# Edge stage of a two-layer graph network: layers spread in eight steps over two rounds, edge batches taken singly by TensorE

## What is computed

```python
def _L0_gnn_ref(node_feats, src, dst, eps, W1, b1, W2, b2, gamma, beta):
    neigh = segment_sum(node_feats[src], dst, num_segments=n)
    h = (1.0 + eps) * node_feats + neigh
    h = relu(h @ W1 + b1) @ W2 + b2          # 256 -> 512 -> 256
    mean, var = h.mean(axis=0), square(h - mean).mean(axis=0)
    return (h - mean) * rsqrt(var + BN_EPS) * gamma + beta
```

## Time and profile before

| | |
|---|---|
| median of three runs | 2266.91 us |
| the profiled execution | 2265.84 us |
| its span | 2264.3 us |
| TensorE matmuls busy / weight loads busy | 93% / 87% |
| VectorE / ScalarE / GpSimd busy | 73% / 54% / 25% |
| edge stage, from the first batch to the last layer | 150.6 to 602 us |

### The profile page before, as it was taken

The page is one execution under the profiler, slowest core; times in us unless marked ns, Lnnn a source line. Parts: engine busy times, 40 slices in busy tenths (PEclk is TensorE's granted clock), DMA queues, the critical chain, the costliest instruction groups (busy, mean ns, idle before and its releaser), DMA issues. The chain is left out here.

```text
span 2264.3 us, 47270 instructions
## 1 busy us (share of the span) xinstructions
PE 2094.6 (93%) x18287; PEld 1966.4 (87%) x18287; DVE 1653.3 (73%) x3119; ACT 1233.8 (54%) x2875; POOL 569.9 (25%) x406
## 2 busy tenths in 40 slices
PE   5559999999879999998999999999999999999996
PEld 3348999999769999997778999899988999999996
DVE  6888877778388888885657655556657867888885
ACT  5565555555437676675533444444435336677674
POOL 3000000000016777773000000000000014777775
PEclk9789999999989999999999999999999999999998
DMA  3413333333547778776001666366651025777776
GB/s 122 142 59 105 102 89 89 112 95 89 160 157 217 222 225 240 222 225 169 20 25 50 184 194 188 98 196 188 188 156 63 20 92 173 226 225 237 232 220 170
DMA packets 241114, 339.04 MB, mean 150 GB/s; under 512 B 33407, under 2 KB 202546, under 8 KB 240754
## 3 DMA queue, kind: packets, MB, share of 16 engines
q1 hardware_dynamic: 208908, 296.19, 41.6%
q0 software_dynamic: 28528, 35.76, 8.5%
q10 hardware_dynamic: 3446, 3.97, 0.5%
HBM read 258.89 MB, written 76.95 MB: 148 GB/s over the span
## 5 line engine op out<-in xcount | busy, mean ns | idle before, releaser
L1977 POOL DMA_INDIRECT SC<-xd,slot_i x128 | 186.5, 1457 | 1461.3 <-DVE slot_q L1613 1332.4
L2371 PE MATMUL bank<-WB_r,XN_r 128*128 128x448 f32 x1400 | 399.7, 367 | 3.7 <-DVE WB_r L2330 3.7
L2330 DVE TENSOR_TENSOR WB_r<-WB,WB_r 128x448 fp32r<-128x448 f32 x350 | 214.0, 624 | 166.1 <-ACT WB_r L2323 166.1
L2323 ACT CAST WB_r<-WB 128x448 fp32r<-128x448 f32 x350 | 197.6, 568 | 222.2 <-PE bank L2371 219.1
L2371 PEld LDWEIGHTS bank<-WB_r,XN_r 128*128 128x128 f32 x1400 | 263.2, 188 | 26.8 <-DVE wb__r L2296 4.4
L1907 PE MATMUL bank<-SC_r,WB_r 128*128 128x256 f32 (+1 forms) x2064 | 250.7, 280 | 8.2 <-issue 7.4
L1907 PEld LDWEIGHTS bank<-SC_r,WB_r 128*128 128x128 f32 x2064 | 244.0, 188 | 12.7 <-issue 12.7
L1048 ACT CAST WB_r<-bank 128x200 fp32r<-128x200 f32 x391 | 140.5, 359 | 194.7 <-PE bank L1032 193.4
L1922 PE MATMUL bank<-R_r,H_r 128*128 128x256 f32 x1752 | 215.1, 282 | 4.8 <-DVE R_r L1818 4.8
L1922 PEld LDWEIGHTS bank<-R_r,H_r 128*128 128x128 f32 x1752 | 208.9, 189 | 5.1 <-issue 5.1
L1770 ACT ACTIVATE wb_<-bank,WB 128x256 f32<-128x256 f32 (+1 forms) x344 | 133.2, 476 | 80.0 <-PE bank L1907 41.3
(11 more groups left out here) (463 smaller groups left out, 5130.4 us busy)
## 6 DMA issues: line engine op xcount, KB each, us to landing
WB<-adjw SPq DMA_DIRECT2D x350, 224.0 KB, 2.9
WB<-in_f_pack SPq DMA_DIRECT2D x127, 512.0 KB
WB<-in_f_pack SPq DMA_DIRECT2D x62, 640.0 KB
adjw<-X SPq DMA_DIRECT2D x24, 1600.0 KB, 7.5
WB<-in_f_pack SPq DMA_DIRECT2D x65, 516.0 KB
xd<-XN SPq DMA_DIRECT2D x15, 640.0 KB, 5.5
y<-X SPq DMA_DIRECT2D x10, 640.0 KB, 3.3
X<-y SPq DMA_DIRECT2D x6, 640.0 KB, 6.5
```

Of the source, the lines that this page charges most:

```text
L1977: e.indirect_dma_start(yin[i % 2][:, q * D:(q + 1) * D], None, XD, bass.IndirectOffsetOnAxis(ap=slot_i[:, 2 * i + q:2 * i + q + 1], axis=0 ...
L2323: e.copy(split_w(m)[0], RAW[m % PR]).then_inc(S("whigh"), 1)
L2330: e.tensor_tensor(al, RAW[m % PR], ah.bitcast(F32), ALU.subtract).then_inc(S("wlow"), 1)
L2371: mm_ = e.matmul(conv_bank(k, band, c)[:, 0:PW], x[st][:, o], y, start=(st == 0 and i == 0), stop=(st == T - 1 and i == 2))
```

## The change

TensorE takes a batch in front of each sums slot, in place of two in front of every other slot. The sixteen matmuls of the layers of a pair of rounds come in eight steps of two: a step of `layer1_pe` behind slots 3, 5 and 7 of the odd round and slot 0 of the next, a step of `layer2_pe` behind slots 3, 5 and 7 of that round and slot 0 of the one after. `layer2_pe` now goes through the four hidden blocks outside and the two output halves inside, so its first two steps need only the first two hidden blocks. `layer1_act` comes in two halves, the second a round later; `layer2_act` and `stats_dve` come a round later.

```diff
-    def layer2_pe(e, q):
+    def layer2_pe(e, q, hc):
         o = pair_cols(q)
         w = o.stop - o.start
-        e.wait_ge(S("lay"), 6 * q + 4)
+        e.wait_ge(S("lay"), 6 * q + (2 if hc < 2 else 4))
         for c in range(2):
-            for hc in range(4):
-                m = e.matmul(B[6][:, c * 256:c * 256 + w], w2[:, hc, c * 128:(c + 1) * 128], hidden[:, hc, 0:w],
-                             start=(c == 0 and hc == 0), stop=(hc == 3), skip_group_check=True)
-        m.then_inc(S("layT"), 1)
+            m = e.matmul(B[6][:, c * 256:c * 256 + w], w2[:, hc, c * 128:(c + 1) * 128], hidden[:, hc, 0:w],
+                         start=(c == 0 and hc == 0), stop=(hc == 3), skip_group_check=True)
+        if hc == 3:
+            m.then_inc(S("layT"), 1)
...
+    PARTS_AT = ((0, 3), (0, 5), (0, 7), (1, 0), (1, 3), (1, 5), (1, 7), (2, 0))
+
+    def layers_pe(e, b, i):
+        for part, (later, at) in enumerate(PARTS_AT):
+            if at == i and layers_at(b - later) is not None:
+                (layer1_pe if part < 4 else layer2_pe)(e, layers_at(b - later), part % 4)
...
     def count_pe(e):
-        for b in range(T + 3):
+        for b in range(T + 5):
             for i in range(8):
-                for j in (i, i + 1) if i % 2 == 0 else ():
+                for j in (i,):
                     if has_batch(b, j):
                         hots_pe(e, 8 * b + j)
                 if i == 1 and 2 <= b < T + 2:
                     turn_sums_pe(e, b - 2)
                 if 1 <= b <= T:
                     sums_pe(e, b - 1, i)
-                if i == 5 and layers_at(b) is not None:
-                    layer1_pe(e, layers_at(b))
-                if i == 7 and layers_at(b) is not None:
-                    layer2_pe(e, layers_at(b))
+                layers_pe(e, b, i)
...
-                if i == 1 and b and layers_at(b - 1) is not None:
-                    layer2_act(e, layers_at(b - 1))
+                if i == 1 and layers_at(b - 2) is not None:
+                    layer2_act(e, layers_at(b - 2))
                 if i == 6 and layers_at(b) is not None:
-                    layer1_act(e, layers_at(b))
+                    layer1_act(e, layers_at(b), 0)
+                if i == 1 and layers_at(b - 1) is not None:
+                    layer1_act(e, layers_at(b - 1), 1)
...
-                if i == 5 and b and layers_at(b - 1) is not None:
-                    stats_dve(e, layers_at(b - 1))
+                if i == 6 and layers_at(b - 2) is not None:
+                    stats_dve(e, layers_at(b - 2))
```

More of the change, by code:

```diff
@@ L1117, in pair_cols, with layer1_pe @@
         return slice(256 * q, min(256 * q + 256, NP))
-    def layer1_pe(e, q):
+    def layer1_pe(e, q, hc):
         o = pair_cols(q)
         w = o.stop - o.start
[L1122 to L1127, removed]
-        for hc in range(4):
[L1129 to L1132, removed]
-                m.then_inc(S("layT"), 1)
@@ L1135, in layer2_pe @@
-    def layer2_pe(e, q):
+        if hc == 0:
+            e.wait_ge(S("gadd"), min(2 * q + 2, T))
+            if q:
+                e.wait_ge(S("lay"), 6 * q)
+            else:
+                e.wait_ge(S("w_late"), W_LATE)
+                e.wait_ge(S("key16"), dve_step(FILLS - 1, 0))
+        for c in range(2):
+            m = e.matmul(B[6 + hc // 2][:, hc % 2 * 256:hc % 2 * 256 + w], w1[:, c, hc * 128:(hc + 1) * 128], XT[:, c, o],
+                         start=(hc % 2 == 0 and c == 0), stop=(c == 1), skip_group_check=True)
@@ L1136, in layer2_pe @@
+        if hc % 2:
+            m.then_inc(S("layT"), 1)
+    def layer2_pe(e, q, hc):
         o = pair_cols(q)
         w = o.stop - o.start
-        e.wait_ge(S("lay"), 6 * q + 4)
+        e.wait_ge(S("lay"), 6 * q + (2 if hc < 2 else 4))
         for c in range(2):
-            for hc in range(4):
-                m = e.matmul(B[6][:, c * 256:c * 256 + w], w2[:, hc, c * 128:(c + 1) * 128], hidden[:, hc, 0:w],
-                             start=(c == 0 and hc == 0), stop=(hc == 3), skip_group_check=True)
@@ L1143, in layer2_pe, with layer1_act @@
-        m.then_inc(S("layT"), 1)
-    def layer1_act(e, q):
+            m = e.matmul(B[6][:, c * 256:c * 256 + w], w2[:, hc, c * 128:(c + 1) * 128], hidden[:, hc, 0:w],
+                         start=(c == 0 and hc == 0), stop=(hc == 3), skip_group_check=True)
+        if hc == 3:
+            m.then_inc(S("layT"), 1)
+    def layer1_act(e, q, half):
         w = pair_cols(q).stop - pair_cols(q).start
-        for hc in range(4):
-            if hc % 2 == 0:
-                e.wait_ge(S("layT"), 3 * q + 1 + hc // 2)
+        e.wait_ge(S("layT"), 3 * q + 1 + half)
+        for hc in (2 * half, 2 * half + 1):
@@ L1169, in layers_at @@
     def layers_at(b):
-        return (b - 3) // 2 if b >= 3 and b % 2 else None
+        return (b - 3) // 2 if b % 2 and 3 <= b < 2 * PAIRED + 3 else None
+    PARTS_AT = ((0, 3), (0, 5), (0, 7), (1, 0), (1, 3), (1, 5), (1, 7), (2, 0))
[3 more added lines that the diff above has]
+                (layer1_pe if part < 4 else layer2_pe)(e, layers_at(b - later), part % 4)
     def count_pe(e):
-        for b in range(T + 3):
+        for b in range(T + 5):
             for i in range(8):
-                for j in (i, i + 1) if i % 2 == 0 else ():
+                for j in (i,):
                     if has_batch(b, j):
@@ L1182, in count_pe @@
                     sums_pe(e, b - 1, i)
-                if i == 5 and layers_at(b) is not None:
-                    layer1_pe(e, layers_at(b))
-                if i == 7 and layers_at(b) is not None:
-                    layer2_pe(e, layers_at(b))
+                layers_pe(e, b, i)
     def count_act(e):
         highs_act(e, 2)
-        for b in range(T + 4):
+        for b in range(T + 6):
             for i in range(8):
@@ L1205, in count_act @@
                     sums_act(e, b - 2)
-                if i == 1 and b and layers_at(b - 1) is not None:
-                    layer2_act(e, layers_at(b - 1))
+                if i == 1 and layers_at(b - 2) is not None:
+                    layer2_act(e, layers_at(b - 2))
                 if i == 6 and layers_at(b) is not None:
-                    layer1_act(e, layers_at(b))
+                    layer1_act(e, layers_at(b), 0)
+                if i == 1 and layers_at(b - 1) is not None:
+                    layer1_act(e, layers_at(b - 1), 1)
     def count_dve(e, d):
         e.tensor_scalar(scalec, epsc, goodc, 1.0, ALU.mult, ALU.add).then_inc(S("xts"), 1)
-        for b in range(T + 5):
+        for b in range(T + 6):
             for i in range(8):
```

## The result

The changed kernel took 2251.67 us (median of six runs, 2247.77 to 2257.96) against 2266.54 us for the kernel before in the same comparison: a ratio of 0.9937, 95% interval 0.9920 to 0.9954, or 14.3 us. The forecast was 2255.8 us, 11.1 us less. Both intervals hold the 11.1. The median itself lies 0.3 us under the forecast's range of 2252 to 2261.5; set on the 2266.91 us that the forecast started from, the ratio 0.9937 gives 2252.6 us and 0.9953 gives 2256.3, both inside.

A forecast was written before the change was run, and what follows sets the result against it. TensorE and VectorE were taken as level in even rounds, their handshake wasting 1.59 us a pair. Gains of 9.3 + 0.8 + 0.2 + 0.8 = 11.1 us gave 2255.8 us, range 2252 to 2261.5.

The forecast's parts named there:

- The bound and its waits: Edge stage, rounds 3 to 22: all 1.59 us of TensorE's waits a pair go; VectorE's slack is 0.46 us.
- What is added: Group starts, batches behind sums and transposes add 0.66 us a pair, steps 0; net gain 0.93 us, 9.3 in ten pairs.
- Rounds 1 and 2: Rounds without layers: gains of 0.8 us in round 1, VectorE still the later engine there, and 0.2 in round 2.
- The end: Last pair's chain of layers: layer 2's first half needs only two relus, so some 0.8 us move ahead.
- Waits that it adds: Counts, transposes, layer 1's input and ScalarE's moves in the edge stage: all covered, costing nothing.
- A: Rival: steps cost at their edges; at 0.10 us each 7.8 us are given back, 2263.6 us. Same 0.05, slower 0.04.
- B: Rival: VectorE still holds TensorE and half of the 1.59 us stays, giving 2263.8 us; chance 0.06.
- C: Rival: all 2.44 us of idle weight loads a pair are waste, giving 2247.3 us; chance 0.03.
- D: Clock rival: the layers' steps run at half clock, pairs last 6.9 us more, 2325 us; chance 0.01.
- The sum: Whole kernel: 9.3 + 0.8 + 0.2 + 0.8 = 11.1 us less, with 1.8 us allowed for scatter between runs.

The follow-up runs named there:

- spread-only kernel: Changed kernel with batches in pairs again, only the layers spread: 2258.68 us, ratio 0.9942 to the kernel before.
- loads on VectorE: VectorE's L1002 comparison cut into eight instructions in three kernels: ratio 1.0275 in the kernel before, 1.0049 in the change, 1.0074 with only the layers spread.
- second profile: The changed kernel run again with no edit: ratio 0.9953 to the kernel before, edge stage 440.36 us.
- step ahead of the sums: Changed kernel with each step of the layers in front of its sums slot rather than behind it: 2262.96 us, ratio 0.9955.

## Why the prediction was right, point by point

**The bound and its waits**: as predicted. All the waits of a pair went; VectorE's slack of 0.46 us a batch was enough with no batch of rounds 3 to 23 over 0.85 us. That the waits came from VectorE being level with TensorE in even rounds, and not from the pairing as such, the spread-only kernel and the loads on VectorE show. Here the prediction was right without having told the halves of the change apart: it asked whether single feeding removes the wait and took its slack from the single batches, where the spread alone leaves 0.13 us.

**What is added**: the net was forecast at 0.93 us a pair and came at 0.94 (34.80 to 33.87), 9.4 us in ten pairs against 9.3. By the terms: six group starts at 0.083, as predicted; transposes 0.04 us dearer each (0.172 against 0.136 on the average), as predicted; batches behind sums or transposes 0.84 to 0.85; steps at 0.86, nothing at their edges. Two small errors cancel in it: the waits were measured against 0.83 us for every batch, though the first batch behind sums takes 0.84 when nothing holds it, so they were 1.54 us and not 1.59, and the additions sum to 0.61 and not 0.66.

**Rounds 1 and 2**: this step was mis-sized. It said 0.8 and 0.2 us. Round 2 gave 0.2; round 1, from batch 8 to batch 16, lasts 15.48 us against 15.53. The timeline of TensorE in the changed kernel shows why:

```profile
166.40 0.24 PE L1027 MATMUL bank<-wb_,SC 128*128 128x100 bf16 x1 [1.45 <-DVE SC L1002]
...
167.78 0.56 PE L1088 MATMUL bank<-H_r,WB_r 128*128 128x256 f32 x1
...
169.21 0.30 PE L1027 MATMUL bank<-SC 128*128 128x100 bf16 x1
...
170.66 0.51 PE L1088 MATMUL bank<-H_r,WB_r 128*128 128x256 f32 x1
```

The first six sums take 1.43 us and not 0.80, and the batches about them 1.38 and 1.45: TensorE comes out of round 0, where it waited for VectorE at each batch, at the lower of its two clocks. The granted clock (the third figure from the end) of the round's first 6.8 us, of the first six sums, and of the next six:

```profile
166.40:173.20 6.80, 6.80 (x96) 6.64 (x96) 6.15 (x13) 3.26 (x13) 0.00 (x0) 0.66 0.84 242
167.78:169.21 1.43, 1.43 (x10) 1.34 (x8) 1.43 (x4) 0.67 (x3) 0.00 (x0) 0.50 1.01 290
170.66:171.59 0.93, 0.93 (x10) 0.88 (x7) 0.75 (x2) 0.62 (x3) 0.00 (x0) 0.83 1.01 290
```

In the kernel before it was 0.75 over the round's first 6.8 us: there two batches, 2.95 us at 0.50, were over before the sums began, and twelve sums took 1.72 us, where twelve later ones took 1.51. The round's eight batches took 7.87 us where they had taken 9.04, and its sums 7.61 where they had taken 6.49. Of these 1.12 us some 0.55 are sums moved forward into the slow clock, 0.33 four more group starts, and 0.21 a wait in front of the batch of 178.37, for which VectorE's L1006 ended at 178.27. The forecast put what would stay down to VectorE; of the 2.1 us by which the round stayed above its 13.4 us of work, VectorE held 0.2 and the slow clock some 1.9. The forecast left the clock out of this term although rows 1 showed 0.59. In the change's second profile the clock rose sooner: the second six sums took 0.81 us and the round 15.30, a gain of 0.2.

**The end**: 0.8 us forecast, 0.7 measured. Timeline of TensorE, the last pair:

```profile
578.37 1.80 PE L1130 MATMUL bank<-XT,wa 128*128 128x128 f32 x14 [1.02 <-ACT XT L1157]
580.23 2.04 PE L1140 MATMUL bank<-wb_,wa 128*128 128x128 f32 x16
```

Layer 2 follows layer 1 without the 0.71 us of idle time; from layer 1's start to layer 2's end there are 3.74 us against 4.63. Some 0.2 us of it go to a longer wait ahead (1.02 against 0.80).

**Waits that it adds**: none showed, on TensorE, for counts, transposes or layer 1's input.

**The rivals**. A fell with the row of a step (0.86 us) and with the step ahead of the sums. B didn't come true in the change, but with 0.49 us more a batch it does: then VectorE sets the pace. C: weight loads are busy for 15.93 of 16.90 us in a round in which TensorE waits at no moment, so the 0.97 us in which they are idle are no wait. The Trainium skill ("Perfetto Trace Analysis", Identifying the Most-Contended Engine) takes their busy share as a measure of TensorE's headroom, beside the share of its peak arithmetic; by that share this stretch would still have 6%, which the trace's starts don't bear out. D: 1.00 throughout rounds 3 to 22.

**The sum**: 11.1 us forecast, 10.35 in the stage, 0.7 us of the difference in round 1. What none of the terms held is the scatter of the rest of the program: 11 us between kernels behind the stage, and once 9 us ahead of it. Its 1.8 us for scatter was too small, by the three runs it rested on; the eleven of one later kernel spread over 8 us. That the first comparison's median came 0.3 us under the range, and the second's ratio on the forecast, is this scatter; the stage is what the forecast can be held to.

## What to carry to other kernels

When two engines hand buffers to each other, compare their work stretch by stretch, not over the stage: waits arise where they are level, and moving a third kind of work into those stretches takes them away without touching the handshake. Read waits from starts against the pace of the same instructions elsewhere, since pipelined durations hide part of a gap. And price each half of a double change alone: here the spread alone shortened the stage by 15.8 us, single feeding alone by 6.6 and both together by 10.4; single feeding, which is robust against a slower partner, cost 5 us of the stage for want of one.

## What the runs showed of the hardware

- A group of fp32 or fp32r matmuls behind small bf16 ones (26 in 0.83 us) starts 0.08 us late, once, whichever of the two kinds it is: six sums and a step take 1.66 us in either order, twelve sums 1.51. Between fp32r sums and fp32 steps, in either order, the switch costs nothing net.
- One bf16 comparison of 1024 columns on VectorE cut into eight takes 1.09 us and not 0.60, 0.49 more: 0.07 us for each further instruction.
- Matmuls kept back to back (16.90 of 16.90 us) left the weight loads idle for 6% of the time (busy 15.93 us).
- The clock stayed low over the first sums after a stretch of waits: six sums at 1.43 us (granted clock 0.50), then 0.93 (0.83), then 0.80 (1.00); in a second profile of the same kernel 1.43, then 0.81.
